# Causal mask of a grouped-query attention: added on VectorE in one pass with the row maximum, in place of mask products on TensorE

## What is computed

```python
q = (h @ Wq).reshape(B, S, 32, 128).transpose(0, 2, 1, 3)      # k, v the same with 8 heads
q, k = apply_rope(q, cos, sin), apply_rope(k, cos, sin)
k, v = jnp.repeat(k, 4, axis=1), jnp.repeat(v, 4, axis=1)
logits = jnp.einsum('bhqd,bhkd->bhqk', q, k) / sqrt(128)
logits = jnp.where(causal, logits, finfo.min)
attn = softmax(logits)
out = einsum('bhqk,bhkd->bhqd', attn, v).transpose(0, 2, 1, 3).reshape(B, S, 4096) @ Wo
```

## Time and profile before

| | |
|---|---|
| median of 3 runs | 2507.11 us (2506.83 to 2512.26) |
| profiled execution, its own time | 2511.31 us |
| its span in the profile | 2509.1 us |
| mean granted TensorE clock | 0.991 of full speed |
| PE busy over the span | 2463.0 us (98%) |
| DVE busy over the span | 1554.4 us (62%) |
| ACT busy over the span | 1397.8 us (56%) |

### The profile page before, as it was taken

How to read it: one execution, slowest core, us unless ns; L and a number is a source line. 1 busy time by engine, 2 the same in 40 slices (tenths; PEclk the granted TensorE clock), 3 DMA queues, 4 the chain that set the end, 5 groups by cost and what they waited for, 6 DMA issues and landing times. The chain is left out here.

```text
span 2509.1 us, 40557 instructions
## 1 busy us (share of the span) xinstructions
PE 2463.0 (98%) x12632; PEld 1856.4 (74%) x12632; DVE 1554.4 (62%) x2796; ACT 1397.8 (56%) x2171; POOL 1155.1 (46%) x1155
## 2 busy tenths in 40 slices
PE   8999999999999999999999999989999999999998
PEld 4677777777777777777776588768888888888876
DVE  6666666666666666666665523276657557566577
ACT  3677777777777777777777423233424324233252
POOL 1556565555555555555555244234334334242331
PEclk8999999999999999999999999999999999999999
DMA  6122222222222222222221322121010010010100
GB/s 215 42 45 53 47 54 45 53 46 53 53 45 53 45 53 45 54 48 55 47 53 41 129 89 88 39 84 43 0 42 17 25 42 17 25 38 4 38 1 34
DMA packets 47612, 125.40 MB, mean 50 GB/s; under 512 B 6033, under 2 KB 23441, under 8 KB 41426
## 3 DMA queue, kind: packets, MB, share of 16 engines
q1 hardware_dynamic: 47570, 124.85, 18.5%
HBM read 80.27 MB, written 10.49 MB: 36 GB/s over the span
## 5 line engine op out<-in xcount | busy, mean ns | idle before, releaser
L427 DVE TENSOR_REDUCE row_max<-ps_max 128x1 f32<-128x512 f32 x1024 | 670.3, 687 | 194.2 <-PE ps_max L517 171.8
L292 POOL TENSOR_TENSOR p_parts<-probs,p_parts 128x1024 f16<-128x1024 f32 x256 | 547.8, 2150 | 365.6 <-ACT p_parts L346 364.7
L341 ACT ACTIVATE probs<-ps_score 128x1024 f32<-128x1024 f32 x512 | 523.5, 1023 | 239.2 <-PE ps_score L533 217.3
L531 PE MATMUL ps_score<-Q,K 128*128 128x512 f32 x1024 | 407.3, 398 | 2.1 <-ACT probs L341 2.1
L533 PE MATMUL ps_score<-Q,K 97*128 97x512 f32 x1024 | 406.7, 397 | 0.0
L517 PE MATMUL ps_max<-KX,Q 68*128 68x512 f32 x1024 | 378.2, 410 | 3.0 <-DVE row_max L427 2.8
L421 DVE TENSOR_TENSOR Q<-ps_x,Q 64x512 fp32r<-64x512 f32 x254 | 175.1, 689 | 242.7 <-ACT Q L336 239.0
L346 ACT ACTIVATE p_parts<-probs 128x1024 f16<-128x1024 f32 x256 | 269.5, 1053 | 4.1
L517 PEld LDWEIGHTS ps_max<-KX,Q 68*128 68x128 f32 x1024 | 189.1, 189 | 76.1 <-issue 28.1
L531 PEld LDWEIGHTS ps_score<-Q,K 128*128 128x128 f32 x1024 | 194.2, 190 | 60.4 <-ACT probs L341 8.6
L1422 POOL CAST q_hi<-roped 128x512 fp32r<-128x512 f32 x64 | 39.1, 612 | 404.1 <-DVE roped L1609 212.3
(11 more groups left out here) (292 smaller groups left out, 4404.1 us busy)
## 6 DMA issues: line engine op xcount, KB each, us to landing
Q<-Q SPq DMA_DIRECT2D x64, 512.0 KB, 4.3
ffn_raw<-in_w_ffn SPq DMA_DIRECT2D x22, 768.0 KB, 4.3
w_raw<-in_w_qrope SPq DMA_DIRECT2D x32, 512.0 KB, 3.7
wq_raw<-in_wq SPq DMA_DIRECT2D x8, 1024.0 KB, 5.7
wo_raw<-in_wo SPq DMA_DIRECT2D x8, 1024.0 KB, 4.8
content_k<-probs SPq DMA_DIRECT2D x8, 512.0 KB, 6.8
Q<-content_q SPq DMA_DIRECT2D x64, 64.0 KB
K<-content_k SPq DMA_DIRECT2D x64, 64.0 KB
```

The lines of the kernel that those rows point to most:

```text
L292: pool.tensor_tensor(p_lo[:, j, :, :], probs[:, j, 0:PAIRED, :], p_hi[:, j, :, :], ALU.subtract)\
L341: act.activation(probs[:, j, 2 * half:2 * half + 2, :], ps_score[half][:, :, :], ACT.Exp, scale=SCALE).then_inc(exped, 1)
L427: dve.tensor_reduce(row_max[:, t, j:j + 1], ps_max[t % 2][:, :], axis=AXX, op=ALU.max)\
L531: pe.matmul(ps_score[half][:, k, :], K1[:, b, t * P:(t + 1) * P], Q1[:, b, j, :], start=True, stop=False)
```

## The change

The mask is no longer a product. A 128 x 512 tile `mask` in SBUF holds zeros, and -1e30 above the diagonal in its last 128 columns; its last n columns fit a row tile of n columns. DVE adds it to the scores, writes minus the sum back into the same PSUM tile, and takes the minimum of what it writes, which is minus the row maximum: one call per row tile in place of the plain reduction. The exponential then reads with `scale=-1.0`. The waits of the DVE call are carried by an increment of a new semaphore, `gate_dve`, once per unit. PE no longer waits for the mask, DVE does once, and POOL's set-up has one select and one cast fewer.

```diff
-        mask = buf("mask_sb", [P, 2, P], F32R)
-        mask_raw = buf("mask_raw", [P, 2, P])
+        mask = buf("mask_sb", [P, S])
...
-            pool.memset(mask_raw[:, :, :], 0.0).then_inc(mask_set, 1)
+            pool.memset(mask[:, :], 0.0).then_inc(mask_set, 1)
             pool.wait_ge(mask_set, 1)
-            pool.affine_select(out=mask_raw[:, 0, :], in_=mask_raw[:, 0, :], compare_op=ALU.not_equal, fill=1.0,
+            pool.affine_select(out=mask[:, S - P:S], in_=mask[:, S - P:S], compare_op=ALU.is_ge, fill=-1e30,
                                base=0, pattern=[[-1, P]], channel_multiplier=1).then_inc(mask_set, 1)
-            pool.affine_select(out=mask_raw[:, 1, :], in_=mask_raw[:, 1, :], compare_op=ALU.is_ge, fill=-1e30,
-                               base=0, pattern=[[-1, P]], channel_multiplier=1).then_inc(mask_set, 1)
-            pool.wait_ge(mask_set, 3)
-            pool.tensor_copy(mask[:, :, :], mask_raw[:, :, :]).then_inc(mask_set, 1)
...
-                    act.activation(probs[:, u % 2, t, 0:n], ps_s[bank][:, at:at + n], ACT.Exp,
+                    act.activation(probs[:, u % 2, t, 0:n], ps_s[bank][:, at:at + n], ACT.Exp, scale=-1.0,
                                    bias=minus_max[:, t:t + 1], accum_out=sums[:, u % 2, t:t + 1]).then_inc(exped, 1)
...
                     if k == 0:
                         dve.wait_ge(scored, i + 1)
+                        dve.sem_inc(gate_dve, 1)
                     bank, at = place[t]
-                    dve.tensor_reduce(minus_max[:, t:t + 1], ps_s[bank][:, at:at + (t + 1) * P], axis=AXX, op=ALU.max,
-                                      negate=True).then_inc(maxed, 1)
+                    n = (t + 1) * P
+                    row = ps_s[bank][:, at:at + n]
+                    dve.tensor_tensor_reduce(out=row, in0=row, in1=mask[:, S - n:S], scale=-1.0, scalar=3e38,
+                                             op0=ALU.add, op1=ALU.min, accum_out=minus_max[:, t:t + 1]).then_inc(maxed, 1)
...
             dve.wait_ge(tables_in, 16)
+            dve.wait_ge(mask_set, 2)
...
                     for k, (q, kk) in enumerate(TERMS):
-                        pe.matmul(out, Q[q][:, b, t * P:(t + 1) * P], K[kk][:, b, 0:n], start=k == 0, stop=False)
-                    last = pe.matmul(ps_s[bank][:, at + n - P:at + n], mask[:, 0, :], mask[:, 1, :],
-                                     start=False, stop=True)
+                        last = pe.matmul(out, Q[q][:, b, t * P:(t + 1) * P], K[kk][:, b, 0:n], start=k == 0, stop=k == 2)
                 last.then_inc(scored, 1)
...
-            pe.wait_ge(mask_set, 4)
-
```

More of the change, by code:

```diff
@@ L1317, in gqa_stage @@
         stored = sem("stored")
-        gate_sp, gate_pool = sb["gate_sp"], sb["gate_pool"]
+        gate_sp, gate_pool, gate_dve = sb["gate_sp"], sb["gate_pool"], sb["gate_dve"]
         first_splits = [([w[:, i] for w in parts], raw[:, i], count)
@@ L2000, in keep @@
             sb[name] = stack.enter_context(nc.sbuf_tensor(name, shape, dt))
-        sb = {name: ctx.enter_context(nc.semaphore(name)) for name in ("gate_sp", "gate_pool")}
+        sb = {name: ctx.enter_context(nc.semaphore(name)) for name in ("gate_sp", "gate_pool", "gate_dve")}
         keep(ctx, "ident", [P, P])
```

## The result

| | before | after |
|---|---|---|
| median | 2506.97 us (4 runs, 2504.96 to 2512.26) | 2485.52 us (4 runs, 2481.24 to 2487.09) |
| ratio | | 0.9903, 95% interval 0.9888 to 0.9917 |
| profiled span | 2509.1 us | 2483.0 us |
| stretch of the units | 776.5 us | 750.4 us |

A forecast was written before the change was run, and what follows sets the result against it. PE's instruction list was taken as the bound, with DVE's loop 0.55 us a unit behind; 26.9 us saved less 7.5 given back made 19.4, so a median of 2488 us, range 2479 to 2504.

The forecast's parts named there:

- What bounds the kernel: Attention: PE's instruction list sets 8.34 us a unit; DVE's loop, maxima through exponentials, scaling and rotation, needs 7.79.
- PE loses 256 products: Score products on PE: removing the masks saves 0.105 us each, 0.42 a unit, 26.9 us over 64 units.
- The accumulator at 0.117 each: DVE's fused maxima: reading the accumulator out into `minus_max` costs an extra 0.117 us per pass.
- x': Time from the start of DVE's maxima until the second exponential may start, after the change; predicted 1.80 us.
- rival 1: DVE's accumulator is free or nearly so, x' up to 1.6: gain 24 to 27 us; chance 0.17.
- the prediction's own formula: Gain is 26.9 - 7 x (6 x (x' - 1.53) - 0.74) - 5 x (x' - 1.53), brackets never below zero.
- Lateness 0.27 a unit: From unit 2 on, DVE's loop of 8.19 us exceeds PE's 7.92, so exponentials fall 0.27 further behind each unit.
- margin of 0.74: At unit 7, scaled probabilities are ready 0.74 us before PE's transpositions need them, in the kernel before.
- 7.5 us given back: PE stalls on DVE: 0.88 us in each of the first 7 key heads, 1.35 in the last.
- The wait of 0.9 us for DVE once per key head: Sign of the forecast: PE shows a 0.9 us wait for DVE's probabilities once per key head.
- Rival 4: DVE's fused pass runs at half rate, x' 2.88: 31 us slower, 2538; chance 0.13 with all other slow cases.
- The sum: Whole kernel: 26.9 us won on PE less 7.5 given back is 19.4 us less, median 2488.

The follow-up runs named there:

- e1: Kernel before with the 256 mask products left out of PE, no mask applied at all; stretch 750.0 us, ratio 0.9905 to the kernel before.
- e4: Kernel before with an extra unused DVE pass of 512 columns in each unit; stretch 781.3 us, ratio 1.0018 to the kernel before.
- e10: Changed kernel with the last addition of each rotation left out on DVE; stretch 749.7 us, ratio 0.9900 to the kernel before.
- e11: Kernel before with each mask product issued twice on PE; stretch 805.1 us, ratio 1.0124 to the kernel before.
- e3: Changed kernel with an extra unused DVE pass of 512 columns in each unit; stretch 787.2 us, ratio 1.0040 to the kernel before.
- e12: Changed kernel with an extra POOL addition of 128x512 beside DVE's scaling in units 1 to 6; stretch 787.4 us, ratio 1.0048 to the kernel before.
- e9: Changed kernel with an extra 512-column DVE pass a unit and each rotation's last addition left out; stretch 750.3 us, ratio 0.9904 to the kernel before.
- e8: Changed kernel with each rotation's last addition moved from DVE to POOL, plus an extra 512-column DVE pass; stretch 817.6 us, ratio 1.0160 to the kernel before.

## Why the prediction was right, and where it was not

- **What bounds the kernel**: right. PE's list, with DVE's loop next to it at 0.55 us a unit. e1 shows the first. e4 shows the second: its loop takes 8.46 us with an extra pass of 0.72, so 7.74 without it, where the prediction has 7.79.
- **PE loses 256 products, 26.9 us**: right. 26.5 measured by e1, and 26.8, or 0.105 each, by e10, in which DVE is never late. The choice of 0.105 and not 0.06 a mask is confirmed from the other side by e11.
- **The accumulator at 0.117 each, x' = 1.80**: too high. x' is 1.55 (the plain maxima have 1.39). The read exists, as an instruction of its own, but it starts together with the next pass; what is left of the surcharge is its 0.14 us once, behind the third pass. The error was to take ACT's spacing and DVE's small instruction as prices of a slot. The case that came true is rival 1 (x' up to 1.6), which had 0.17. The gain at its upper edge, by the prediction's own formula, is 26.5 us and not the 24 written there.
- **Lateness 0.27 a unit, 1.62 us at unit 7 against a margin of 0.74**: that lateness adds up from unit to unit and is paid at unit 7 is right; where it comes from is not. With x' = 1.55 the prediction's own loop needs 7.94 us by its sum and 7.91 by e3 (8.63 less the 0.72 of the extra pass), against PE's 7.93, and next to nothing would have added up. The measured 7.98 stand in e1 as well, with plain maxima, and come from a term that the prediction lacked: once PE's unit is as short as 7.93, DVE's scaling meets POOL's subtraction (1.34 to 1.36 us in units 2 to 6, 1.54 in unit 1, for 1.27). Unit 7 is late by 0.66 in the changed kernel and by 0.48 in e1, so the fused pass has 0.18 of it. In both kernels PE starts 0.06 us after the scaling of unit 7. That the lateness fills the margin of 0.74 and hardly overdraws it is luck for the change, as the forecast had no term for its cause.
- **7.5 us given back**: 0.4 to 0.7 measured (against e1 and e10). This is the term that makes the forecast of the gain too small. The wait of 0.9 us for DVE once per key head, by which the prediction meant to be recognised, does not appear; PE is held for 0.1 us there.
- **Slope**: the formula takes 47 us off the gain per us of loop; e3 (0.65 us, 36.8 us lost) gives 57. The three falls of the clock account for 3.7 us, which leaves 51; the rest is not accounted for.
- **Rival 4, half rate**: not so, 0.692 us at 512 columns. One source lies in PSUM, so the sentence of the Trainium skill, "Vector Engine (DVE) Microarchitecture Reference", section "Points that are easy to get wrong", that the prediction draws on does not strike by its letter, and no run here shows the case that it speaks of.
- **The sum**: 19.4 us predicted, 26.1 in the profile, 21.5 by the medians, 24.3 by the ratio (20.8 to 28.1). The predicted 2488 is near the median 2485.5 partly by luck: the medians moved by less than the profiled stretch, and the stretch is the measure that isolates the change.

## What to carry to other kernels

In this kernel work taken off a saturated TensorE paid by the distance between starts, successor included (0.105 us a product), not by its own slot (0.06). Before moving work onto an engine "with room", find its longest chain per round, waits for its own results included: here 62% busy meant 0.55 us of room in 8.34, and the next pass would have cost more than the change won. Check who else touches SBUF at the moments that the move shifts: here the shorter unit alone, with DVE's work unchanged, brought POOL's passes on top of DVE's scaling. And leave one half of the change out at a time: only e1 shows that the lateness in the changed kernel is not the price of the fused pass.

## What the runs showed of the hardware that was not expected

- The accumulator read of the fused DVE pass lasts 0.142 us and starts with the next pass; the fused pass starts its successor 0.61, 0.51 to 0.52 and 0.25 us later at 512, 384 and 128 columns.
- DVE's scaling of 1280 columns, SBUF to SBUF, takes 1.27 us alone, 1.34 to 1.69 with a short overlap with a POOL pass, and 2.13 to 2.30 beside a whole one. POOL's other passes kept their 1.27 to 1.29 us in e12. Where DVE's pass came first, POOL paid: in e9 POOL's subtraction, begun 0.15 us after DVE's extra addition, took 1.69 us and not 1.29, and DVE's addition its usual 0.68.
- TensorE's clock fell to its lower level for 3.4 us after PE had been busy for 1.49 of 3.30 us (e3), and the key head took 1.2 us more. After waits of similar length in e12 (1.22 and 0.59 us at unit 7) it did not fall.
- An addition of 128x512 with both sources in SBUF took 0.69 us next to an idle POOL, and 1.33 beside POOL's addition (e8):

```profile
1894.90 1.33 DVE L1613 TENSOR_TENSOR spare<-by_sin 128x512 f32<-128x512 f32 x1
```
